# Moving first-batch queries and keys between two SBUF tensors directly instead of through DRAM, and changing the order of small work where one stage follows another

## What is computed

```python
def _L0_cond_ref(x, c, Wc, bc, ...):
    c6 = jax.nn.silu(c) @ Wc + bc
    sh_msa, sc_msa, g_msa, sh_mlp, sc_mlp, g_mlp = jnp.split(c6, 6, axis=-1)
    xm = _modulate(_ln(x), sh_msa, sc_msa)
    q = (xm @ Wq + bq).reshape(B, S, NH, DH)      # k, v alike
    w = jax.nn.softmax(jnp.einsum('bqhc,bkhc->bhqk', q / DH, k), axis=-1)
    y = jnp.einsum('bhqk,bkhc->bqhc', w, v).reshape(B, S, H)
    x = x + g_msa[:, None, :] * (y @ Wo + bo)
    xm2 = _modulate(_ln(x), sh_mlp, sc_mlp)
    h = jax.nn.gelu(xm2 @ W1 + b1, approximate=False)
    x = x + g_mlp[:, None, :] * (h @ W2 + b2)
```

## Time and profile before

| | before |
|---|---|
| median of 3 runs | 929.71 us (926.41 to 933.15) |
| the profiled execution, as timed | 927.77 us |
| its span, from the first to the last instruction | 925.6 us |
| mean granted TensorE clock, as a share of full speed | 0.989 |
| PE, DVE, ACT, POOL busy | 878.1, 587.9, 518.9, 468.7 us |

### The profile page before, as it was taken

The page is one execution under the profiler, slowest core; times in us unless marked ns, Lnnn a source line. Parts: engine busy times, 40 slices in busy tenths (PEclk is TensorE's granted clock), DMA queues, the critical chain, the costliest instruction groups (busy, mean ns, idle before and its releaser), DMA issues.

```text
span 925.6 us, 14715 instructions
## 1 busy us (share of the span) xinstructions
PE 878.1 (95%) x5294; PEld 539.3 (58%) x5294; DVE 587.9 (64%) x916; ACT 518.9 (56%) x955; POOL 468.7 (51%) x614
## 2 busy tenths in 40 slices
PE   5999999999989999998999999999999999999997
PEld 3453444444347779776878775444444433687874
DVE  4687887788895366554533277878777886234323
ACT  2226878776784444444364441677866778744331
POOL 4393565564748645447544424748255016665330
PEclk9979999999999999999999999999999999999999
DMA  7565584666212030123214136546636531100001
GB/s 231 153 160 163 155 248 121 183 173 186 85 57 91 1 134 1 36 72 139 79 48 180 12 95 173 154 127 184 177 112 200 138 108 58 38 14 1 23 24 45
DMA packets 67087, 101.30 MB, mean 109 GB/s; under 512 B 19644, under 2 KB 30984, under 8 KB 66632
## 3 DMA queue, kind: packets, MB, share of 16 engines
q1 hardware_dynamic: 58584, 86.90, 31.6%
q0 software_dynamic: 5920, 10.90, 4.6%
q10 hardware_dynamic: 2512, 2.58, 1.1%
HBM read 64.65 MB, written 35.02 MB: 108 GB/s over the span
## 4 chain that ended last, share of the span: by engine, by line
PE 78%; DVE 10%; ACT 4%; issue 4%; POOL 3%; DMA 0%; SPq 0%; DVEq 0%; POOLq 0%; ACTq 0%
PE PS L1151 13%; PE PS L715 12%; PE PS L689 12%; PE PS L1133 12%; PE PS L644 5%; PE PS L700 4%; PE PS L625 3%; PE PS L620 3%; DVE U L877 3%; ACT PH L779 2%; PE PS L456 2%; PE PS L657 2%; PE PS L633 1%; PE PS L474 1%; PE PS L1269 1%
## 5 line engine op out<-in xcount | busy, mean ns | idle before, releaser
L877 DVE TENSOR_REDUCE U<-PS 128x2 f32<-128x1024 f32 x256 | 307.8, 1220 | 55.3 <-PE PS L700 53.7
L779 ACT ACTIVATE PH<-PS 128x512 f32<-128x512 f32 x512 | 275.4, 605 | 87.8 <-PE PS L689 84.8
L689 PE MATMUL PS<-UR 50*128 50x512 f32 x512 | 187.4, 456 | 9.3 <-ACT PH L779 4.6
L700 PE MATMUL PS<-UR 48*128 48x512 f32 x512 | 190.9, 469 | 5.4 <-DVE U L877 4.7
L1199 POOL TENSOR_TENSOR PHR<-PH,PHR 128x512 fp32r<-128x512 f32 x96 | 124.1, 1296 | 118.6 <-ACT PHR L1189 118.6
L689 PEld LDWEIGHTS PS<-UR 50*128 50x128 f32 x512 | 79.2, 186 | 147.2 <-ACT PH L779 84.6
L1151 PE MATMUL PS<-UR,PHR 128*128 128x256 f32 x768 | 158.6, 290 | 4.1 <-POOL PHR L1199 4.0
L715 PE MATMUL PS<-PH,U 128*32 128x512 f32 x1024 | 137.2, 608 | 0.3 <-ACT PH L779 0.3
L1151 PEld LDWEIGHTS PS<-UR,PHR 128*128 128x128 f32 x768 | 124.6, 189 | 21.5 <-issue 18.5
L1151 PE MATMUL PS<-W2R,PHR 128*128 128x256 f32 x384 | 108.1, 282 | 0.0
L1188 ACT ACTIVATE PH<-PS,col 128x512 f32<-128x512 f32 x64 | 43.9, 687 | 93.5 <-PE PS L1133 93.5
(11 more groups left out here) (254 smaller groups left out, 1351.2 us busy)
## 6 DMA issues: line engine op xcount, KB each, us to landing
UR<-d_parts SPq DMA_DIRECT2D x112, 192.0 KB, 4.2
d_parts<-UR SPq DMA_DIRECT2D x42, 256.0 KB
d_parts<-UR POOLq DMA_DIRECT2D x40, 256.0 KB, 5.4
d_o<-U SPq DMA_DIRECT2D x32, 256.0 KB, 2.9
U<-in_L_cond_W_dram SPq DMA_DIRECT2D x8, 1024.0 KB, 7.6
W<-in_L_cond_W_dram SPq DMA_DIRECT2D x24, 256.0 KB, 3.3
U<-d_o SPq DMA_DIRECT2D x32, 128.0 KB
U<-d_rec SPq DMA_DIRECT2D x16, 256.0 KB
```

Of the source, the lines that this page charges most:

```text
L689: self.close(pe.matmul(dst, KP[g // 2][r:r + SROWS + 2, j, kt * P:(kt + 1) * P], QP[g // 2][r:r + SROWS + 2, j, :], start=True, stop=True) ...
L700: ins = pe.matmul(bank(2 + (w + 2) % 4), QP[g // 2][r:r + SROWS, j, qt * P:(qt + 1) * P], KP[g // 2][r:r + SROWS, j, :], start=True, stop= ...
L779: nc.scalar.activation(PH[:, m % 2, j, :], self.where("ST", n), ACT.Exp).then_inc(self.a_free, 1)
L877: v.tensor_reduce(mx[:, G % 2, :].rearrange("p (r c) -> p r c", r=2)[:, :, c // 2], PS[:, 2 + (w + 1) % 4:4 + (w + 1) % 4, :], AX.X, ALU.m ...
```

## The change

1. For the first batch, groups 0 and 1 of queries and keys no longer go through DRAM. A new `fill_first` issues transfers from the split parts directly into the slots, one per head and slot: 16 rows of 512 numbers each. For queries SP issues 12 for group 0 and 12 for group 1; for the keys of group 0 ACT issues 6 and POOL 6; for the keys of group 1 POOL issues 12. Groups 2 and 3 keep the DRAM route (POOL saves, SP fills). Counts and waits on semaphores follow.
2. `mod_turn` stands ahead of the spins, and there are 3 spins in place of 9.
3. The S5 factors and powers leave the attention tail. Factors and `(1, 8)` stand at the start of `mlp0_dve`, `(8, 64)` and `(64, 511)` after the statistics of batch 2.
4. The MLP norm of batch 1 is made at the end of the attention, in both attentions: statistics at step 230, `norm_pool` at step 246. The chain on POOL at q = 1 and the four ACT operations at q = 3 are gone from both MLPs, and so are the statistics at the start of both DVE sequences.
5. `GB` of batch 3 goes from step 252 to step 202.
6. At two places in `mlp0_dve`, `dve_turned` goes ahead of `norm_stats`.

```diff
@@ attention_schedule
-            put(64 * b + 60, "GB", b, 0)
+            put(64 * b + 60 if b < 3 else 202, "GB", b, 0)
+    put(230, "MLS", 1, 0)
+    put(246, "MLN", 1, 0)
     put(228, "MLT", 0, 0)
-    put(236, "S5F", 0, 0)
-    put(243, "S5F", 1, 0)
-    put(247, "S5F", 2, 0)
-    put(251, "S5F", 3, 0)
...
@@ pe
+                if self.a == 0:
+                    mod_turn(pe, 2, 3, 6)
                 self.spin(pe, self.spins)
                 for n in self.steps(self.pe_task(pe)):
...
-                    elif n == LEAD:
-                        mod_turn(pe, 2, 3, 6)
...
-                            if self.first(b) and g == 1:
-                                pe.wait_ge(first_filled, FILLS)
+                            if self.first(b) and g == 0:
+                                pe.wait_ge(first_filled, 6 * 16)
+                            elif self.first(b) and g == 1:
+                                pe.wait_ge(self.stored[0], 12 * 16)
...
@@ pool_task
+                    elif self.first(b) and (kind, i) == ("FILL", 0):
+                        self.fill_first(pool, 0, "K", first_filled, (0,))
                     elif self.first(b) and (kind, i) == ("FILL", 1):
-                        pool.wait_ge(self.filled[0], self.parts_filled(0, 0))
+                        self.fill_first(pool, 1, "K", self.stored[0])
                         self.save_parts(pool, "WQ", b, 1)
                         self.save_parts(pool, "WK", b, 1)
-                        self.fill(pool, b, i, "K")
...
+            def fill_first(self, eng, g, c, done, rows=(0, 1)):
+                k = int(c == "K")
+                eng.wait_ge(self.split[0], k + 1)
+                for slot, part in enumerate(SLOTS[c]):
+                    for r in rows:
+                        for j in range(2):
+                            h = HD * (4 * g + r + 2 * j)
+                            r0 = 64 * r + HD * slot
+                            eng.dma_start((KD if k else QD)[0][r0:r0 + HD, 2 * g + j, :],
+                                          parts_d[k][h:h + HD, part, :]).then_inc(done, 16)
...
-        att0, att1 = Attention(0, 9), None
+        att0, att1 = Attention(0, 3), None
...
@@ mlp0_act
-            if q == 3:
-                norm_apply(act, "m0", 1)
-            elif q == 6:
+            if q == 6:
                 mlp0.act_turned(act, 1)
@@ mlp0_pool
-            if q == 1:
-                norm_chain(pool, link, "m0", 1)
@@ mlp0_dve
-            norm_stats(v, link, ln("m0", 1), 1, [(att0.xd, 2 * TT)])
+            s5_factors(v, link)
+            s5_powers(v, link, (1, 8))
             att0.dve_task(v, link)(*att_tail(att0, "RCP", 0))
...
             norm_stats(v, link, ln("m0", 2), 2, [(att0.xd, 3 * TT)])
+            s5_powers(v, link, (8, 64))
+            s5_powers(v, link, (64, T - 1))
...
+            mlp0.dve_turned(v, 2)
             norm_stats(v, link, ln("s", 0), 0, [(mlp0.xd, 1)])
-            mlp0.dve_turned(v, 2)
...
+            mlp1.dve_turned(v, 0)
             norm_stats(v, link, ln("s", 2), 2, [(mlp0.xd, 3)])
-            mlp1.dve_turned(v, 0)
```

More of the change, by code:

```diff
@@ L134 @@
              ("m1", 2), ("m1", 3)] + [("a1", b) for b in range(B)] + [("m2", b) for b in range(B)])
-ACT_LN = [k for k in LN_ORDER if k[0] in ("s", "m1") or k[0] in ("m0", "m2") and k[1] or k in (("a1", 0), ("a1", 1))]
+ACT_LN = [k for k in LN_ORDER if k[0] in ("s", "m1") or k[0] in ("m0", "m2") and k[1] > 1 or k in (("a1", 0), ("a1", 1))]
 def ln(stage, b):
@@ L723, in task @@
                         norm_apply(act, "a1", b)
-                    if self.first(b) and (kind, i) == ("WK", 0):
-                        self.save_parts(act, kind, b, i)
-                    elif self.first(b) and (kind, i) == ("FILL", 0):
-                        self.fill(act, b, i, "K")
+                    if self.first(b) and (kind, i) == ("FILL", 0):
+                        self.fill_first(act, 0, "K", self.filled[0], (1,))
                     elif self.first(b) and kind == "MROW":
@@ L807, in task @@
                         self.mlp.dve_turned(v, 0, high=True)
-                    elif kind == "S5F" and self.a == 0:
-                        if b == 0:
-                            s5_factors(v, link)
-                        else:
-                            s5_powers(v, link, ((1, 8), (8, 64), (64, T - 1))[b - 1])
                     elif kind == "MLS":
-                        norm_stats(v, link, self.mlp.norm0, 0, [(self.xd, TT)])
+                        norm_stats(v, link, self.mlp.norm0 + b, b, [(self.xd, TT * (b + 1))])
                     elif kind == "V" and not self.on_act(kind):
@@ L889, in task @@
                     elif kind == "MLN":
-                        norm_pool(pool, link, self.mlp.norm0, 0, [self.turned(B - 1)])
+                        norm_pool(pool, link, self.mlp.norm0 + b, b, [(self.mlp.t_full, 2) if b else self.turned(B - 1)])
                     elif kind == "S5N" and self.a == 0:
@@ L965, in parts_saved @@
                 if self.a:
-                    return self.saved[i], 96 * (b + 1) + (128 + 96 * (quarter if b == 0 else 1) if i == 0 else 0)
+                    return self.saved[i], 96 * (b + 1) + (96 * (quarter if b == 0 else 1) if i == 0 else 0)
                 if b:
-                    return self.stored[i], 96 * b + 64 * i
-                return (self.saved[0], 64 * (1 + quarter)) if i == 0 else (self.stored[1], 64)
+                    return self.stored[i], 96 * b + (192, 64)[i]
+                return self.stored[1], 64
             def save_parts(self, eng, kind, b, i, quarter=0):
@@ L978, in save_parts, with wait_moved @@
                             (self.stored if self.a == 0 and (b or i) else self.saved)[i], 16)
+            def fill_first(self, eng, g, c, done, rows=(0, 1)):
[8 more added lines that the diff above has]
+                                          parts_d[k][h:h + HD, part, :]).then_inc(done, 16)
+            def wait_moved(self, eng, i, b):
+                if (self.a, i, b) == (0, 0, 0):
+                    eng.wait_ge(first_filled, 6 * 16)
+                    eng.wait_ge(self.stored[0], 12 * 16)
+                    for g in range(2):
+                        eng.wait_ge(self.filled[g], self.parts_filled(0, g))
+                else:
+                    eng.wait_ge(*self.parts_saved(i, b))
             def fill(self, eng, b, g, kinds="QK"):
@@ L986, in fill @@
                     src = d_parts[self.a, 4 * b + 2 * (g // 2) + k]
-                    done = first_filled if self.first(b) and (c, g) == ("K", 1) else self.filled[g]
                     for r in range(2):
@@ L992, in fill @@
                                           src[s0:s1].rearrange("s d h t -> (s d) h t")[
-                                              :, 4 * (g % 2) + r:4 * (g % 2) + 4:2, :]).then_inc(done, 16)
+                                              :, 4 * (g % 2) + r:4 * (g % 2) + 4:2, :]).then_inc(self.filled[g], 16)
             def parts_filled(self, b, g):
-                return FILLS * (self.b0 + b + 1) + (FILLS if g != 1 else 0)
+                return FILLS * (self.b0 + b) + FIRST_FILLED[g]
             def maxima(self, eng, G):
@@ L1009, in task @@
                     if kind in ("WQ", "WK"):
-                        if self.a or (b, kind, i) == (0, "WQ", 0):
+                        if self.a:
                             self.save_parts(sp, kind, b, i)
+                    elif self.first(b) and kind == "FILL" and i < 2:
+                        self.fill_first(sp, i, "Q", self.filled[i])
                     elif kind == "FILL":
-                        if (b, i) == (0, 1):
+                        if (self.a, b, i) == (1, 0, 1):
                             self.save_parts(sp, "WQ", 0, 0, 1)
                             self.save_parts(sp, "WK", 0, 0, 1)
-                        self.fill(sp, b, i, "Q" if self.first(b) and i < 2 else "QK")
+                        self.fill(sp, b, i)
                     elif kind == "MROW" and not self.first(b):
```

14 lines of the change are left out of this document (5 added, 9 removed).

## The result

The changed kernel takes 915.27 us (median of 6 runs, 912.62 to 920.23) where the kernel before took 929.07 beside it (6 runs, 924.18 to 933.15). The ratio is 0.9855, with a 95% interval of 0.982 to 0.989: 13.5 us faster, between 10 and 17. The forecast was 916 with 909 to 924.

The account below looks back on a forecast made before the run. TensorE (PE) was taken as the bound, with time to gain only where it idles or runs slow: lead-in and stage joins. -3.7 -5.6 -1.0 -1.3 = -11.6 us from 927.8 gives 916; range 909 to 924.

Parts of the forecast that it names:

- The range of 913 to 920: Whole kernel: the forecast's own time range in us, said to follow from the ends of its terms; chance 0.50.
- Direct transfers and spins: Lead-in: group 0 lands at 34.4, first maximum at about 35.0 instead of 38.74; -3.7 us (ends -4.4 and -1.8).
- Hidden by 3.9 us: Lead-in: SP's queries of group 1 land at 41.9, PE needs them around 45.8, so they cost nothing.
- Start of the first MLP: PE's waits of 1.10, 0.79 and 2.32 go and full clock saves 1.4 behind them; together -5.6 us.
- First swap: Turned norm ahead of statistics at 322.53: PE's 1.77 wait goes, 0.8 given back; -1.0 us (ends -1.77 and 0).
- Second swap: Same swap at 395.80: takes most of PE's 1.49 wait, no PE wait for DVE follows; -1.3 us.
- At no price: Norm of batch 1 in second attention costs at most 0.25 us; GB of batch 3 at step 202 under 1 us.
- Late transfers: Rival, lead-in: direct transfers bring group 0 only at 38.2, first maximum stays where it was; 920 us, chance 0.14.
- The new wait that keeps half: Rival, first MLP: a new wait takes half the gain, 2.8 of 5.6 us stays; 919 us, chance 0.12.
- The better-clock rival: Rival, 42 to 50 us: earlier columns keep PE supplied and clock up, 3.4 us more saved; 913 us, chance 0.10.
- The worse one: Rival, lead-in: without six spins PE idles, the clock falls earlier, costing 3.4 us; 920 us, chance 0.10.
- The slower rival: Rival, lead-in: SP's issues cost 1.33 us each (no gain) or 1.7 (937 us) instead of 0.68; chance 0.04.

Follow-up runs that it names:

- the two profiles with full clock from 34 to 56 us: Second profiles of both kernels, each unchanged and run once more: kernel before 924.63 us, changed kernel 916.80 us (one execution each).
- the seven profiles with this lead-in: Changed kernel, its repeat and five edits of it elsewhere, all with three spins, early modulation transposes and shared issue; 915.27 to 924.90 us.
- b: Kernel before with the direct route alone, keeping nine spins, the transposes behind them and the old joins; 930.15 us (one execution).
- the second profiles: Both kernels run once more unchanged for a second profile: kernel before 924.63 us, changed kernel 916.80 us (one execution each).
- e: Changed kernel with the S5 factors and powers back in the attention tail; 923.57 us (7 executions), ratio 0.9929 to the kernel before.
- the three runs with one long wait before the first scores: Changed kernel with groups 0 and 1 through DRAM (924.80 us), transposes behind the three spins (919.61), or SP alone issuing group 0's direct transfers (924.73).

## Why the prediction was right, point by point

**The sum.** Forecast -11.6, measured -13.5 with an interval of -10 to -17. From the two profiles with full clock from 34 to 56 us the parts are -5.4, -5.35, -0.95, -0.15 and -0.14, together -12.0. But the first of these is not firm. At the end of attention 0 the seven profiles with this lead-in stand between -4.8 and -8.9, -6.6 in the mean, and the two of the kernel before at 0 and -3.3, so there the lead-in is worth about -4.9 and the sum is about -11.5. That this meets -11.6 is in part luck: the lead-in brought 1.2 us more than forecast and the second swap 1.2 less, and of the start of the first MLP 1.3 us are clock that b kept without the edit. A part of the measured -13.5 is clock too. The executions with clock on record have a median span of 926.4 us for the kernel before (23 of them) and 913.9 for the changed one (7); each span less the share that was not granted gives medians of 915.9 and 906.5. By this estimate some 9 us of the 12.5 between the spans are gained at equal clock, and about 3 come with more clock. The range of 913 to 920, said to follow from the ends, is 914.7 to 919.1 by them.

**Direct transfers and spins, forecast -3.7.** The step held, the size was low. ACT's transfers began at 25.99, not 26.9, and were issued at 29.97, not 31.0: the first scores came at 33.4 instead of 34.4, the first maximum at 34.05 instead of 35.0, so -4.7 (-4.6 between the second profiles). The landing was not what was off. Over all 48 transfers it took 2.6 us in the median, counted from the start of the issue, but the last of group 0, for which PE waits, landed 3.4 us after the end of its issue (3.35 in the second profile), as in the sum. The Trainium skill's 2.0 us for a fixed cost ("DMA: Bandwidth & Descriptors", section "Anatomy of one DMA — SWDGE (gpsimd) path") gave 33.0, nearer to 33.4 than my 34.4, but by luck: it was added to an issue that ended 1.0 us earlier than assumed, and 3.4 us is what the trace has for that landing. The other 0.8 of the 5.4 lies behind it, where PE waited 2.71 us for group 1 before and 1.62 now.

**"Hidden by 3.9 us", the queries of group 1.** This step failed. In five of the seven runs with this lead-in PE waited 0.98 to 2.48 us for them at 43.5 to 45.2. The last of them was there at 42.9 to 45.2, not 41.9: its issue ended up to 3.0 us late, and it landed up to 6.6 us after that instead of 3.4. In the five with a wait PE was ready at 41.9 to 43.3, not 45.8, since the 49.5 that I started from stood behind 6.8 us of low clock; in the second profile of before PE was ready at 47.45. It cost no gain because the DRAM route made PE wait too, which the first profile did not show; I had taken "no wait" there as a fact of the kernel.

**Start of the first MLP, forecast -5.6.** Close, -5.34, with all three waits gone and the clock at 1.00 over 276 to 284. The 1.4 for the clock has its size (1.32 in b), but its reason, PE's pause, is not shown: b has the same pause and full clock. What I missed is that small DVE operations take up to 1.3 us each beside POOL; so the first powers end late, `mrow_f` stands behind them, and 0.85 of what the second product had won (-13.2 at its second step) went back.

**First swap, forecast -1.0.** Measured -0.95.

**Second swap, forecast -1.3.** Measured -0.13. The sentence that failed is "no PE wait for DVE follows": true for DVE, but POOL waits for those statistics in front of a low part that PE needs. I named what stood behind the statistics on DVE, not what stood behind them on POOL.

**At no price.** The norm in the second attention -0.14, right. In the first it costs 0.47, which the forecast did not have.

**The rivals.** Late transfers did not happen (group 0 at 33.4). The new wait that keeps half fell, though e shows that it is real when the table stays. The better-clock rival was seen in the second profile, with full clock from 34 to 56, but the second profile of the kernel before has the same, so it is no gain of the edit. The worse one was not seen in either profile of the changed kernel, whose clock stayed up until 45 at least; it followed in the three runs with one long wait before the first scores. The slower rival rests on SP's price of an issue, which was 0.72 and not 1.33. That the mechanism is real shows h: 24 issues by SP instead of 12 put the start back by 9 us, and its one execution took 924.73 us.

## What to carry to other kernels

Two things that end together must be removed together: here spins and the route, neither of which alone moved the first scores. When an instruction is moved ahead of another on one engine, follow both outputs to every engine that queues for them, since the wait that goes may come back one engine further on. When a transfer is waited for as the last of many, take the landing of the last ones and not the median. Profile a kernel twice before a lead-in is read to the microsecond, and compare positions stage by stage instead of spans.

## What the runs showed of the hardware

Direct transfers within SBUF of 16 rows of 2 KB land 1.9, 2.6 and 6.0 us after the start of their issue (minimum, median, maximum), where fills from DRAM took 2.7, 3.4 and 5.7. Issuing took 0.72 us each on SP, 0.49 on POOL and 0.66 on ACT, on average. A DVE operation on 2 columns took 1.32 us beside POOL operations on 512 columns, and 0.23 us where POOL was idle. With the same PE work up to 42 us, to 0.1 us, one execution had the clock at its lower level (1.2 of 2.4 GHz) for much of the next 14 us, and another not at all; this moved the second pass by 2.9 us. Behind the same three waits at the start of the first MLP the clock was at its lower level for 3.4 us in two executions and at full speed in a third, which was worth 1.3 us.
